# One transpose of K per step of an attention loop, moved from TensorE to VectorE and to transfers inside SBUF

## The chip, the cores and the metric

The kernel runs on one core of one Trainium2 chip. The metric is the device time of one execution in microseconds, the median of several runs: 2669.0 us before the change (three runs, 2667.27 to 2669.63 us).

## The reference, cut to what matters

The input is 2 x 1024 tokens of width 512, in float32. A block of linear attention with decay (32 heads of 128) and a gated feed-forward block follow one another, each between layer norms and with a residual. The attention part, as the reference has it:

```python
qkv = jax.nn.silu(hidden_states @ qkv_w.T)
...
def step(kv, blk):
    cq, ck, cv = blk
    scores = jnp.einsum('bhnd,bhmd->bhnm', cq, ck) * diag_decay
    intra = jnp.einsum('bhnm,bhmd->bhnd', scores, cv)
    inter = jnp.einsum('bhnd,bhde->bhne', cq * q_decay, kv)
    kv_next = kv * block_decay + jnp.einsum('bhnd,bhne->bhde', ck * k_decay, cv)
    return (kv_next, intra + inter)
...
normed = norm_w * xf.astype(attn.dtype)
gate = jax.nn.sigmoid(hidden_states @ gate_w.T)
return gate * normed @ out_w.T
```

K enters twice. The scores need it with the head's dimension on the partitions, as the projection leaves it. The state `kv_next` sums over the tokens of a block, so there K must have the tokens on the partitions: it has to be transposed, and scaled by `k_decay`.

## The kernel before, in words

**Tiling.** The heads go in 16 pairs, the 2048 tokens in four segments of 512 (`NSEG`, four chunks of 128 each). A pair with a segment is a step, `a`; there are 64. All engines are programmed by hand: each has its own list, with semaphores between them, and the order below is the order of each list. Loops over the pairs are hardware loops whose body holds four steps (`four_steps(i, ...)`, called i-th turn here, with `j` 0 to 3).

**TensorE** (`step`, L1260) interleaves step `a`'s attention with the projections of step `n = a + 1`. A projection is a `unit(n, seg, u)`, 12 matmuls of 512 columns or 24 of 256: units 0 and 1 make K of the two heads, 2 and 3 Q, 4 and 5 V, 6 and 7 the gate. The order in a step is: transposes and scores of head 0, unit 0, transposes and scores of head 1, unit 1, `contributions` (the new states, from `kd` and V), units 2 and 3, `attend` of both heads, units 4, 5 and 6, two `project_out`, unit 7, two more `project_out`. In `transposes_and_scores` (L1195) four 128x128 transposes of `k` go to the PSUM bank `kt_at[h]`, and then the four score matmuls follow. The same bank takes the attention output in `attend` (L1216) later in the step.

**ScalarE** (`step`, L548): `k_decay` (L532) copies `kt_at` with the decay as its scale into `kd`; then come the sigmoids of units 0 to 3 (`sigmoid`, L511), `square` (L538) of the two heads' attention outputs into `sq`, `gated_hi`, and the sigmoids of units 4 to 7. In each turn's step `j` = 3, `split_out_hi` stands between the squares and `gated_hi`.

**VectorE** (`step`, L860): `decay_scores` and `silu` of units 0 and 1 by turns, `update_state` of both heads, `silu` of 2 and 3, `gate` (L850, waits on the square), `silu` of 4 and 5, and `add_out` four times.

**GpSimd** (`attention`, L359): `query_decay`, `add_squares` (reads `sq`), `gated_lo` (the low half of the gated output, which `project_out` needs), in `j` = 3 also `split_out_lo` (L331), for which the first `project_out` of that step waits.

**SyncE** issues the transfers: four weight blocks, a table and the output weights for each pair (L259 to L290), each when its buffer has come free.

The last three steps (`late_step`, and the beginning of `last_step_and_ffn`) are written out apart and carry the middle layer norms besides; then the feed-forward part follows.

What a unit waits for is set here (L1174 to L1177): the V units wait for `silu` of the Q units, unit 6 for `silu` of unit 4, unit 7 for that of unit 5:

```python
                if u < 2:
                    wait(pe, sig_done, 8 * n - 1 + u)
                else:
                    pe.wait_ge(silu_done, 6 * n + u - 1)
```

Of the kernel before, what the change touches and what calls it, by code (L numbers as in the profile page):

```python
# [21 lines left out]
P = 128  # L22
# [23 lines left out]
CHECKS_PER_PAIR = 3  # L46
CHECK_PAIRS = WIDTH_CHECKS // CHECKS_PER_PAIR
F32R_EXACT = 2.0 ** 12

# [19 lines left out]
def sandwich_kernel(nc, x, w_attn, w_out, norm_w, tables, w_ints, ffn_scales, down_s, out):  # L69
    ctx = ExitStack()  # L70
    with ctx:
# [30 lines left out]
        nw = sb("nw", [P, 2])  # L102
        table = sb("table", [P, TAB])
# [8 lines left out]
        kt_at = [bank("kt_at0"), bank("kt_at1")]  # L112
        sc_st = [bank("sc_st0"), bank("sc_st1")]
        yp = [bank("yp0"), bank("yp1")]
        ln1_ring = kt_at + sc_st + yp
# [21 lines left out]
        kt_done = sem("kt_done")  # L137
# [68 lines left out]
        sumsq = sb("sumsq", [P, TOK], scope=two)  # L206
        two.close()
# [22 lines left out]
        ffn_ps = [proj_ps[0], proj_ps[1], kt_at[0], kt_at[1]]  # L230
# [11 lines left out]
        def chunk(c):  # L242
            return slice(c * P, (c + 1) * P)

# [13 lines left out]
        def _(sp):  # L258
# [25 lines left out]
            with sp.Fori(1, PAIRS) as p:  # L284
                attn_weights(p, KK)
                attn_weights(p, QQ)
                pair_tables(p)
                pair_out_weights(p)
                attn_weights(p, VV)
                attn_weights(p, GG)  # L290
# [12 lines left out]
            for s in range(NSEG):  # L303
                sp.wait_ge(proj_done, 8 * (STEPS - NSEG + s + 1))
                sp.dma_start(xres[s], x_tiles[s]).then_inc(xres_in[s], 16)
# [172 lines left out]
        def _(act):  # L478
# [53 lines left out]
            def k_decay(a, h):  # L532
                act.wait_ge(kt_done, 2 * a + h + 1)
                wait(act, contrib_done, 2 * a + h - 1)
                act.activation(kd[:, h].rearrange("p c d -> p (c d)"), kt_at[h][:, :], ACT.Copy,
                               scale=table[:, TAB_K + h:TAB_K + h + 1]).then_inc(kd_done, 1)

            def square(a, h):  # L538
                act.wait_ge(attn_done, 2 * a + h + 1)
                wait(act, ss_done, 2 * a + h - 1)  # L540
                act.activation(sq[:, h], kt_at[h][:, :], ACT.Square).then_inc(sq_done, 1)  # L541
# [218 lines left out]
        def _(dve):  # L760
# [89 lines left out]
            def gate(a, h):  # L850
                dve.wait_ge(sq_done, 2 * a + h + 1)
                dve.wait_ge(sig_done, 8 * a + 7 + h)
                dve.tensor_tensor(g[:, h], kt_at[h][:, :], g[:, h], ALU.mult).then_inc(gated_done, 1)
# [44 lines left out]
            for s in range(1, NSEG):  # L898
                silu(0, 2 * s - 2)
                silu(0, 2 * s - 1)  # L900
                if s == 1:
                    dve.wait_ge(x_in[3], 16)
                    norm_statistics(y_tile(3), 3)
# [61 lines left out]
            def late_step(a, seg, s):  # L965
# [7 lines left out]
                silu(n, 1)  # L973
                norm_scales(norm_a[s])
# [170 lines left out]
        def _(pe):  # L1145
# [70 lines left out]
            def attend(a, odd, h):  # L1216

                pe.wait_ge(qd_done, 2 * a + h + 1)
                pe.wait_ge(state_done, states_before(a, odd) + (h + 1) * (CH - odd))
                for c in range(CH):  # L1220
                    inter = c > 0 or odd
                    last = pe.matmul(kt_at[h][:, chunk(c)], v[:, c, h], pd[:, h, c],  # L1222
                                     start=True, stop=not inter)
                    if inter:
                        last = pe.matmul(kt_at[h][:, chunk(c)], state[:, h, (c - 1) % CH],  # L1225
                                         qd[:, h, chunk(c)], start=False, stop=True)
# [33 lines left out]
            def step(a, seg, n, pair_n=None, pair_a=None):  # L1260
                odd = seg % 2
                seg_n = (seg + 1) % NSEG
                transposes_and_scores(a, 0)
                unit(n, seg_n, 0, pair_n)
                transposes_and_scores(a, 1)
# [16 lines left out]
            def late_step(a, seg, s):  # L1282
# [3 lines left out]
                transposes_and_scores(a, 0)  # L1286
                unit(n, seg + 1, 0)
                sums_of_squares(s, yp[0])
                transposes_and_scores(a, 1)
# [74 lines left out]
            def last_step_and_ffn(narrow):  # L1364
# [11 lines left out]
                transposes_and_scores(last, 0)  # L1376
# [3 lines left out]
                transposes_and_scores(last, 1)  # L1380
# [109 lines left out]
```

## Time and profile before

| | before |
|---|---|
| median of three runs | 2669.0 us (2667.27 to 2669.63) |
| span of the profiled execution | 2665.3 us; its own time beside the span isn't listed, the median lies 3.7 us above the span |
| TensorE matmuls busy | 2616.9 us, 98% |
| TensorE weight loads busy | 2270.1 us, 85% |
| VectorE | 1095.1 us, 41% |
| ScalarE | 814.2 us, 31% |
| GpSimd | 849.6 us, 32% |
| granted TensorE clock | 0.995 of full speed on the mean |
| 16 DMA engines | 83.61 MB, 31 GB/s on the mean |

The span is the time from the first to the last instruction on the core. Busy time of matmuls is a sum in which neighbours overlap, so the share says that TensorE is hardly ever without work, not what one matmul costs: the cost of one is read from the distance of the starts, or from the chain of waits, in which each piece begins where the piece before it ends. All times of the trace count from the span's start.

### The profile page before, as it was taken

The page shows a single profiled execution, that of the slowest core. Times are in us where ns is not written, and L with a number is a line of the kernel's source. Part 1 is how long each engine was busy: PE and PEld are TensorE (multiplying, and loading weights), DVE is VectorE, ACT ScalarE, POOL GpSimd, SP SyncE. Part 2 cuts the span into 40 slices and gives each one's busy share as a digit, 9 for nine tenths or more (in the row PEclk, how much of TensorE's full clock was granted, in tenths as well). Part 3 has the DMA queues.
Part 4 walks back from the last instruction along what each step waited for, and adds up shares of the span by engine and source line. Part 5 has one row for each costly group of instructions (what it writes and reads, how often), then busy time and mean ns, then how long its engine had stood idle before and what let it go on. Part 6 is the DMA issues. An engine that isn't in the chain of part 4 may idle for free.

```text
span 2665.3 us, 40249 instructions
## 1 busy us (share of the span) xinstructions
PE 2616.9 (98%) x15072; PEld 2270.1 (85%) x15072; DVE 1095.1 (41%) x1945; ACT 814.2 (31%) x1251; POOL 849.6 (32%) x585
## 2 busy tenths in 40 slices
PE   7999999999999999999999999999999999999996
PEld 6888888888888888888888888888888888877774
DVE  6333333333333333333333333333333334655558
ACT  5232223222322222222223232222222224743333
POOL 3232333232323323232323332323223133434345
PEclk9999999999999999999999999999999999999998
DMA  3010101010100001010101010101000011101001
GB/s 127 17 40 17 36 17 40 17 40 17 40 17 29 24 11 39 17 40 17 40 13 40 17 40 17 40 17 37 20 20 25 9 48 32 53 24 40 32 24 63
DMA packets 31985, 83.61 MB, mean 31 GB/s; under 512 B 6096, under 2 KB 6096, under 8 KB 30928
## 3 DMA queue, kind: packets, MB, share of 16 engines
q1 hardware_dynamic: 25776, 70.07, 7.9%
q10 hardware_dynamic: 6048, 11.01, 1.4%
q8 instruction: 148, 2.42, 0.4%
q14 instruction: 13, 0.11, 0.0%
HBM read 76.87 MB, written 4.19 MB: 30 GB/s over the span
## 4 chain that ended last, share of the span: by engine, by line
PE 87%; issue 5%; POOL 3%; DVE 3%; ACT 2%; DMA 0%; POOLq 0%; SPq 0%; ACTq 0%; DVEq 0%
PE proj_ps L1157 54%; PE yp L1157 14%; PE sc_st L1202 4%; PE kt_at L1222 4%; PE kt_at L1225 4%; PE sc_st L1212 4%; PE kt_at L1199 2%; POOL h_lo L413 2%; PE kt_at L1157 1%; DVE stats L764 1%; POOL d_lo L408 0%; DVE y L1095 0%; ACT y L489 0%; POOL f_lo L403 0%; ACT L530 0%
## 5 line engine op out<-in xcount | busy, mean ns | idle before, releaser
L1157 PE MATMUL proj_ps<-x_hi,w_hi 128*128 128x512 f32 x1536 | 623.6, 406 | 1.7 <-DVE x_lo L799 1.4
L1157 PE MATMUL proj_ps<-x_hi,w_lo 128*128 128x512 f32 x1536 | 607.0, 395 | 0.0
L1157 PE MATMUL proj_ps<-x_lo,w_hi 128*128 128x512 f32 x1536 | 606.2, 395 | 0.0
L350 POOL TENSOR_TENSOR sumsq<-sumsq,sq 128x512 f32<-128x512 f32 x128 | 164.4, 1284 | 1234.0 <-ACT sq L541 1233.7
L858 DVE TENSOR_TENSOR y<-yp,y 128x512 f32<-128x512 f32 x256 | 176.9, 691 | 475.9 <-PE yp L1157 475.9
L1157 PEld LDWEIGHTS proj_ps<-x_hi,w_lo 128*128 128x128 f32 x1536 | 289.0, 188 | 68.9
L1157 PEld LDWEIGHTS proj_ps<-x_hi,w_hi 128*128 128x128 f32 x1536 | 290.1, 189 | 59.3 <-DVE x_lo L799 1.8
L1157 PEld LDWEIGHTS proj_ps<-x_lo,w_hi 128*128 128x128 f32 x1536 | 290.3, 189 | 57.7
L1157 PE MATMUL proj_ps<-w_hi,x_hi 128*128 128x256 f32 x1024 | 293.5, 287 | 2.0 <-DVE q L824 2.0
L1157 PE MATMUL proj_ps<-w_hi,x_lo 128*128 128x256 f32 x1024 | 288.3, 282 | 0.0
L1157 PE MATMUL proj_ps<-w_lo,x_hi 128*128 128x256 f32 x1024 | 287.7, 281 | 0.0
L341 POOL TENSOR_TENSOR qd<-q,table 128x512 f32<-128x512 f32 x128 | 162.7, 1293 | 226.2 <-DVE table L808 218.4
L824 DVE TENSOR_TENSOR k<-proj_ps,k 128x512 f32<-128x512 f32 x128 | 88.4, 691 | 312.0 <-ACT k L530 312.0
L1157 PE MATMUL yp<-ow_lo,g_hi 128*128 128x512 f32 x512 | 201.1, 393 | 0.0
L1157 PE MATMUL yp<-ow_hi,g_hi 128*128 128x512 f32 x512 | 200.7, 392 | 0.0
L1157 PE MATMUL yp<-ow_hi,g_lo 128*128 128x512 f32 x512 | 200.6, 392 | 0.0
L530 ACT ACTIVATE g<-proj_ps 128x512 f32<-128x512 f32 x128 | 76.6, 598 | 402.4 <-PE proj_ps L1157 402.4
L824 DVE TENSOR_TENSOR v<-proj_ps,v 128x512 f32<-128x512 f32 x128 | 88.5, 692 | 268.3 <-ACT v L530 268.2
L1157 PEld LDWEIGHTS proj_ps<-w_hi,x_hi 128*128 128x128 f32 x1024 | 192.9, 188 | 2.3 <-issue 2.3
L1157 PEld LDWEIGHTS proj_ps<-w_lo,x_hi 128*128 128x128 f32 x1024 | 193.0, 188 | 0.0
L1157 PEld LDWEIGHTS proj_ps<-w_hi,x_lo 128*128 128x128 f32 x1024 | 192.7, 188 | 0.0
L530 ACT ACTIVATE q<-proj_ps 128x512 f32<-128x512 f32 x128 | 76.3, 598 | 363.7 <-PE proj_ps L1157 363.6
(122 smaller groups left out, 4368.3 us busy)
## 6 DMA issues: line engine op xcount, KB each, us to landing
raw<-w_attn SPq DMA_DIRECT2D x64, 512.0 KB, 3.3
check<-w_ints ACTq DMA_DIRECT2D x42, 256.0 KB, 2.7
ow<-w_out SPq DMA_DIRECT2D x16, 512.0 KB, 3.3
fraw<-w_ints SPq DMA_DIRECT2D x7, 1024.0 KB, 4.8
table_stage<-tables SPq DMA_DIRECT2D x16, 258.0 KB, 2.7
x_again<-x SPq DMA_DIRECT2D x4, 1024.0 KB, 5.1
draw<-w_ints SPq DMA_DIRECT2D x7, 512.0 KB, 3.2
y<-x SPq DMA_DIRECT2D x3, 1024.0 KB, 11.2
```

What stands on the lines that cost most here:

```text
L341: pool.tensor_tensor(qd[:, h].rearrange("p (c n) -> p c n", c=CH), q[:, h].rearrange("p (c n) -> p c n", c=CH), decay.unsqueeze(1).to_broa ...
L350: pool.tensor_tensor(sumsq[:, tokens(seg)], sumsq[:, tokens(seg)], sq[:, h], ALU.add).then_inc(ss_done, 1)
L413: pool.tensor_tensor(h_lo[par][:, t], hid[:, t], h_hi[par][:, t].bitcast(F32), ALU.subtract).then_inc(hlo_done, 1)
L530: act.activation(dst, src, ACT.Sigmoid).then_inc(sig_done, 1)
L824: dve.tensor_tensor(dst, proj_ps[h][:, :], dst, ALU.mult).then_inc(silu_done, 1)
L858: dve.tensor_tensor(tile, yp[t % 2][:, :], tile, ALU.add).then_inc(yacc_done, 1)
L1157: last = pe.matmul(psum, s, m, start=n == 0, stop=n == len(terms) - 1)
L1199: last = pe.transpose(kt_at[h][:, chunk(c)], k[:, h, chunk(c)], ident[:, :])
L1202: last = pe.matmul(sc_st[h][:, chunk(c)], k[:, h, chunk(c)], q[:, h, chunk(c)], start=True, stop=True)
L1212: last = pe.matmul(sc_st[h][:, chunk(c)], kd[:, h, c], v[:, c, h], start=True, stop=True)
L1222: last = pe.matmul(kt_at[h][:, chunk(c)], v[:, c, h], pd[:, h, c], start=True, stop=not inter)
L1225: last = pe.matmul(kt_at[h][:, chunk(c)], state[:, h, (c - 1) % CH], qd[:, h, chunk(c)], start=False, stop=True)
```

## The change

K's four transposes a head leave TensorE, 512 instructions of 128x128 in the whole program. In their place:

- VectorE turns each head's `k` by 32x32 blocks (`turn_blocks`, two instructions of 128x512 a step), behind `silu` of unit 1 and ahead of `update_state`, one step earlier than `kd` is used. The result, `kt`, is a view of the buffer `sq`, which is free at that time.
- SyncE issues sixteen transfers a step (`swap_blocks`), each of 32 partitions x 1 KB from `kt` to a new tile `k_tok`, which put the turned blocks into their block row. Each block row of the destination has its semaphore, `kt_in[b]`.
- ScalarE's `k_decay` reads `k_tok` in SBUF in place of the PSUM bank, and waits for all sixteen transfers, once a step. `square` of head 0 also waits for them, since it overwrites `sq`, out of which they read: for those of step `a + 1`, which were issued in the same step.
- On TensorE the wait for `gated_done` moves from the scores to `attend`. The bank `kt_at` is now `at_ps`, and holds the attention output alone.
- The order of SyncE's weight transfers is written anew around the swaps. SBUF's scratch area for DMA descriptors is halved.

```diff
+        k_tok = sb("k_tok", [P, QUADS, 2, CH, QUAD])
...
+        kt = sq[:, :, :].rearrange("p h n -> p (h n)").rearrange("p (b h c d) -> p b h c d",
+                                                                   b=QUADS, h=2, c=CH)
...
+            def swap_blocks(n):
+                sp.wait_ge(blocks_done, 2 * n + 2)
+                wait(sp, kd_done, 2 * n)
+                for b in range(QUADS):
+                    for i in range(QUADS):
+                        sp.dma_start(k_tok[quad(b), i], kt[quad(i), b]).then_inc(kt_in[b], 16)
+
+            def four_steps(i, more):
+                for j in range(NSEG):
+                    swap_blocks(4 * i + 2 + j)
+                    if j == 1:
+                        attn_weights(i + 1, VV)
+                        attn_weights(i + 1, GG)
+                        if more:
+                            attn_weights(i + 2, KK)
+                            attn_weights(i + 2, QQ)
+                    if j == 3 and more:
+                        pair_tables(i + 2)
+                        pair_out_weights(i + 2)
...
             def k_decay(a, h):
-                act.wait_ge(kt_done, 2 * a + h + 1)
+                if h == 0:
+                    for b in range(QUADS):
+                        act.wait_ge(kt_in[b], 16 * QUADS * (a + 1))
                 wait(act, contrib_done, 2 * a + h - 1)
-                act.activation(kd[:, h].rearrange("p c d -> p (c d)"), kt_at[h][:, :], ACT.Copy,
+                act.activation(kd[:, h].rearrange("p c (i d) -> p i c d", i=QUADS), k_tok[:, :, h],
+                               ACT.Copy,
                                scale=table[:, TAB_K + h:TAB_K + h + 1]).then_inc(kd_done, 1)
 
             def square(a, h):
                 act.wait_ge(attn_done, 2 * a + h + 1)
                 wait(act, ss_done, 2 * a + h - 1)
+                if h == 0 and not (isinstance(a, int) and a == STEPS - 1):
+                    for b in range(QUADS):
+                        act.wait_ge(kt_in[b], 16 * QUADS * (a + 2))
...
+            def turn_blocks(n, h):
+                dve.wait_ge(silu_done, 6 * n + h + 1)
+                if h == 0:
+                    wait(dve, ss_done, 2 * (n - 1))
+                    if isinstance(n, int) and n == 1:
+                        for b in range(QUADS):
+                            dve.wait_ge(kt_in[b], 16 * QUADS)
+                dve.transpose(kt[:, :, h],
+                              k[:, h].rearrange("p (c b t) -> p b c t", c=CH, b=QUADS))\
+                    .then_inc(blocks_done, 1)
...
                 for h in range(2):
                     decay_scores(a, h)
                     silu(n, h)
+                turn_blocks(n, 0)
+                turn_blocks(n, 1)
                 update_state(a, odd, 0)
                 update_state(a, odd, 1)
...
-            def transposes_and_scores(a, h):
+            def scores(a, h):
                 pe.wait_ge(silu_done, 6 * a + 3 + h)
-                wait(pe, gated_done, 2 * a + h - 1)
-                for c in range(CH):
-                    last = pe.transpose(kt_at[h][:, chunk(c)], k[:, h, chunk(c)], ident[:, :])
-                last.then_inc(kt_done, 1)
                 for c in range(CH):
                     last = pe.matmul(sc_st[h][:, chunk(c)], k[:, h, chunk(c)], q[:, h, chunk(c)],
                                      start=True, stop=True)
...
             def attend(a, odd, h):
 
                 pe.wait_ge(qd_done, 2 * a + h + 1)
+                wait(pe, gated_done, 2 * a + h - 1)
...
     nc = bacc.Bacc("TRN2", target_bir_lowering=False, num_devices=1,
+                   dynamic_dma_scratch_size=DMA_SCRATCH)
```

The same turn and swap are also written for the first steps (`swap_blocks(0)`, `swap_blocks(1)`) and the late ones.

**Order on TensorE**, in the loop over the pairs, at the scores of head 1 of a step. Before:

```order
L1157 MATMUL proj_ps0<-x_lo,w_hi 128x512
L1157 MATMUL proj_ps0<-x_hi,w_lo 128x512
L1196 REGISTER_ALU
L1199 MATMUL kt_at1<-ident,k 128x128 x4
L1202 MATMUL sc_st1<-q,k 128x128 x4
L1157 MATMUL proj_ps1<-x_hi,w_hi 128x512
```

and with the change:

```order
L1217 MATMUL proj_ps0<-x_lo,w_hi 128x512
L1217 MATMUL proj_ps0<-x_hi,w_lo 128x512
L1256 REGISTER_ALU
L1258 MATMUL sc_st1<-q,k 128x128 x4
L1217 MATMUL proj_ps1<-x_hi,w_hi 128x512
L1217 MATMUL proj_ps1<-x_lo,w_hi 128x512
```

The four transposes between unit 0 and the scores are gone, and nothing has come in their place. (`x4` counts matmuls of the program; the chip runs each float32 score matmul as two, so the trace has eight.)

**Order on VectorE**, in the same loop, from `silu` of unit 1 on, with the change:

```order
L862 REGISTER_ALU
L865 TENSOR_TENSOR k<-proj_ps,k 128x512
L869 ISA
L875 STREAM_TRANSPOSE sq<-k 128x4x128
L869 REGISTER_ALU
L875 STREAM_TRANSPOSE sq<-k 128x4x128
L64 ISA
L899 SCALAR_TENSOR_TENSOR state<-state,table,sc_st 128x128
```

Before, the row of the state followed that of `k` directly. The two turns are put ahead of six (in steps of the other parity eight) small instructions of `update_state`.

**Order on SyncE**, the beginning of its loop over the pairs with the change (here `sq` is the buffer under the view `kt`):

```order
L321 UNCONDITIONAL_BRANCH
L321 ISA
L300 DMA k_tok<-sq 32x256 x16
L296 ISA
L300 DMA k_tok<-sq 32x256 x16
L64 ISA
L272 ISA
L272 DMA raw<-w_attn 128x1024
```

Seven transfers a pair have become seventy-one, and the sixteen of one step stand without another instruction between them.

## Rows read from the trace of the kernel before

**Rows 1.** The page's busy time; busy time by windows, of the steady steps (PE, PEld, DVE, ACT, POOL).

```profile
PE 2616.9 (98%) x15072; PEld 2270.1 (85%) x15072; DVE 1095.1 (41%) x1945; ACT 814.2 (31%) x1251; POOL 849.6 (32%) x585
...
66.60:2146.00 2079.40, 2079.40 (x12402) 1825.72 (x12400) 758.15 (x1352) 562.58 (x895) 622.45 (x427) 1.00 0.09 27
```

**Rows 2.** The groups of instructions by line: K's transposes (count, busy, mean ns, idle).

```profile
L1199 PE MATMUL kt_at<-ident,k 128*128 128x128 f32 x512 | 76.9, 272 | 0.2 <-issue 0.2
```

**Rows 3.** The chain of waits through one steady step (start us, us, what).

```profile
1012.01 0.44 PE kt_at L1199 x4
1012.44 0.89 PE sc_st L1202 x8
...
1016.13 1.34 PE sc_st L1212 x12
1017.47 5.60 PE proj_ps L1157 x24
...
1026.65 8.47 PE proj_ps L1157 x60
1035.12 2.76 PE yp L1157 x12
```

**Rows 4.** VectorE's copies of the table (ns min/median/max, first and last start us).

```profile
L808 DVE COPY table<-table_stage x16: 421/429/5437, 43.9 to 2181.5; 128x516 f32<-128x516 f32 x16
```

**Rows 5.** VectorE in order of time, around silu of unit 1 of that step.

```profile
1016.80 0.69 DVE L824 TENSOR_TENSOR k<-proj_ps,k 128x512 f32<-128x512 f32 x1 [2.73 <-ACT k L530]
1017.41 2.25 DVE L846 SCALAR_TENSOR_TENSOR state<-state,table,sc_st 128x128 f32<-128x128 f32 x6
```

**Rows 6.** SyncE's issues in order of time; two groups of transfers (KB, us to landing).

```profile
0.75 1.81 SPq L274 DMA_DIRECT2D y<-x  x4
...
2146.58 0.34 SPq L301 DMA_DIRECT2D fraw<-w_ints  x1
2146.97 0.43 SPq L302 DMA_DIRECT2D fs_stage<-ffn_scales  x1
...
raw<-w_attn SPq DMA_DIRECT2D x64, 512.0 KB, 3.3
out<-y SPq DMA_DIRECT2D x8, 256.0 KB, 2.0
y<-x SPq DMA_DIRECT2D x4, 256.0 KB, 3.3
```

**Rows 7.** ScalarE and GpSimd in the same step, from the squares to the low half.

```profile
1024.90 0.60 ACT L541 ACTIVATE sq<-kt_at 128x512 f32<-128x512 f32 x1 [1.19 <-PE kt_at L1225]
1026.68 0.60 ACT L541 ACTIVATE sq<-kt_at 128x512 f32<-128x512 f32 x1 [1.19 <-PE kt_at L1225]
1029.53 0.60 ACT L530 ACTIVATE v<-proj_ps 128x512 f32<-128x512 f32 x1 [0.77 <-PE proj_ps L1157]
...
1025.57 1.27 POOL L350 TENSOR_TENSOR sumsq<-sumsq,sq 128x512 f32<-128x512 f32 x1 [13.91 <-ACT sq L541]
1028.60 2.53 POOL L356 TENSOR_TENSOR g_lo<-g,g_hi 128x512 fp32r<-128x512 f32 x2
```

**Rows 8.** The next step (`j` = 3): ScalarE's squares, GpSimd's low half of the output weights.

```profile
1060.65 0.60 ACT L541 ACTIVATE sq<-kt_at 128x512 f32<-128x512 f32 x1 [0.96 <-PE kt_at L1225]
1062.22 0.60 ACT L541 ACTIVATE sq<-kt_at 128x512 f32<-128x512 f32 x1 [0.97 <-PE kt_at L1225]
...
1066.86 2.39 POOL L333 TENSOR_TENSOR ow_lo<-ow,ow_hi 128x1024 fp32r<-128x1024 f32 x1
```

**Rows 9.** The two late steps: silu of unit 1, and what follows it.

```profile
2226.09 0.69 DVE L824 TENSOR_TENSOR k<-proj_ps,k 128x512 f32<-128x512 f32 x1 [2.72 <-ACT k L530]
...
2235.96 0.60 ACT L541 ACTIVATE sq<-kt_at 128x512 f32<-128x512 f32 x1 [1.19 <-PE kt_at L1225]
...
2264.97 0.69 DVE L824 TENSOR_TENSOR k<-proj_ps,k 128x512 f32<-128x512 f32 x1 [2.73 <-ACT k L530]
2266.49 0.18 DVE L791 RECIPROCAL rstd<-stdev 128x4 f32<-128x4 f32 x1 [0.83 <-ACT stdev L482]
```

More of the change, by code:

```diff
@@ L46 @@
 CHECKS_PER_PAIR = 3
+QUAD = 32
+QUADS = P // QUAD
 CHECK_PAIRS = WIDTH_CHECKS // CHECKS_PER_PAIR
 F32R_EXACT = 2.0 ** 12
+DMA_SCRATCH = 8192
 ACT = mybir.ActivationFunctionType
@@ L111, in sandwich_kernel @@
         proj_ps = [bank("proj_ps0"), bank("proj_ps1")]
-        kt_at = [bank("kt_at0"), bank("kt_at1")]
+        at_ps = [bank("at_ps0"), bank("at_ps1")]
         sc_st = [bank("sc_st0"), bank("sc_st1")]
         yp = [bank("yp0"), bank("yp1")]
-        ln1_ring = kt_at + sc_st + yp
+        ln1_ring = at_ps + sc_st + yp
         x_in = [sem(f"x_in{s}") for s in range(NSEG)]
@@ L136, in sandwich_kernel @@
         proj_done = sem("proj_done")
-        kt_done = sem("kt_done")
+        blocks_done = sem("blocks_done")
+        kt_in = [sem(f"kt_in{b}") for b in range(QUADS)]
         score_done = sem("score_done")
@@ L229, in sandwich_kernel @@
         xres = [x_again[:, :, s * SEG:(s + 1) * SEG] for s in range(NSEG)]
-        ffn_ps = [proj_ps[0], proj_ps[1], kt_at[0], kt_at[1]]
+        ffn_ps = [proj_ps[0], proj_ps[1], at_ps[0], at_ps[1]]
         ffn_ps_first = [proj_ps[0], proj_ps[1], yp[0], yp[1]]
@@ L243, in chunk, with quad @@
             return slice(c * P, (c + 1) * P)
+        def quad(b):
+            return slice(b * QUAD, (b + 1) * QUAD)
         norm_a = [NSEG + 2 * s for s in range(NSEG)]
@@ L283, in _ @@
             pair_out_weights(0)
[L284 to L290, printed above, removed]
+            def swap_blocks(n):
[16 more added lines that the diff above has]
+                        pair_out_weights(i + 2)
+            swap_blocks(0)
+            attn_weights(1, KK)
+            attn_weights(1, QQ)
+            pair_tables(1)
+            swap_blocks(1)
+            pair_out_weights(1)
+            with sp.Fori(0, PAIRS - 2) as i:
+                four_steps(i, True)
+            four_steps(PAIRS - 2, False)
             def ffn_weights(n):
@@ L303, in _ @@
             for s in range(NSEG):
+                if s >= 2:
+                    swap_blocks(STEPS - 4 + s)
                 sp.wait_ge(proj_done, 8 * (STEPS - NSEG + s + 1))
@@ L900, in _ @@
                 silu(0, 2 * s - 1)
+                if s == 1:
+                    turn_blocks(0, 0)
+                    turn_blocks(0, 1)
                 if s == 1:
@@ L973, in late_step @@
                 silu(n, 1)
+                turn_blocks(n, 0)
+                turn_blocks(n, 1)
                 norm_scales(norm_a[s])
@@ L1221, in attend @@
                     inter = c > 0 or odd
-                    last = pe.matmul(kt_at[h][:, chunk(c)], v[:, c, h], pd[:, h, c],
+                    last = pe.matmul(at_ps[h][:, chunk(c)], v[:, c, h], pd[:, h, c],
                                      start=True, stop=not inter)
                     if inter:
-                        last = pe.matmul(kt_at[h][:, chunk(c)], state[:, h, (c - 1) % CH],
+                        last = pe.matmul(at_ps[h][:, chunk(c)], state[:, h, (c - 1) % CH],
                                          qd[:, h, chunk(c)], start=False, stop=True)
@@ L1262, in step @@
                 seg_n = (seg + 1) % NSEG
-                transposes_and_scores(a, 0)
+                scores(a, 0)
                 unit(n, seg_n, 0, pair_n)
-                transposes_and_scores(a, 1)
+                scores(a, 1)
                 unit(n, seg_n, 1, pair_n)
@@ L1285, in late_step @@
                 wait(pe, xlo_done, TILES + CH * s)
-                transposes_and_scores(a, 0)
+                scores(a, 0)
                 unit(n, seg + 1, 0)
                 sums_of_squares(s, yp[0])
-                transposes_and_scores(a, 1)
+                scores(a, 1)
                 unit(n, seg + 1, 1)
@@ L1375, in last_step_and_ffn @@
                 pe.wait_ge(xlo_done, TILES + 2 * CH)
-                transposes_and_scores(last, 0)
+                scores(last, 0)
                 sums_of_squares(2, yp[0])
@@ L1379, in last_step_and_ffn @@
                 project(0, 0, ffn_ps_first)
-                transposes_and_scores(last, 1)
+                scores(last, 1)
                 contributions(last, 1, 0)
```

6 lines of the change are left out of this document (3 added, 3 removed).

## Prediction

> **What bounds the kernel now.** First the busy times. TensorE is busy 98% of the span, and in the window of the steady steps all 2079.4 of 2079.4 us; no other engine passes 41% [rows 1]. So what TensorE does not have to do shortens the program, as long as nothing it waits for comes late. Second the cost of the thing removed. The group of K's transposes gives 272 ns for one, 512 of them [rows 2]. That is a duration with overlap in it. The chain of waits, whose pieces don't overlap, gives 0.44 us for the four of one head, ahead of 0.89 us for eight score matmuls [rows 3]. Third, the idle time ahead of that group is 0.2 us in all [rows 2]: no wait hides in it. Fourth, since the new path runs over four engines, the time at which each wants its input, from the timelines of one steady step.
>
> **What is taken from TensorE.** 64 steps x 2 heads x 0.44 us = 56.3 us. It would be less if the scores, now straight behind a unit, began later than the transposes do. The contributions stand behind a unit already: twelve matmuls in 1.34 us, 0.112 each, and the scores behind the transposes take 0.111 each [rows 3]. So the change of neighbour costs nothing that shows; I allow 54 to 59 us. The wait for the gated output that moves to attend costs nothing: that output belongs to the step before, whose projections out of it are done by then.
>
> [...]
>
> **What VectorE gets.** Two turns of 128x512 a step, which this trace doesn't have. The nearest rows are a copy of 516 elements (0.43 us at the median) and a product of 512 (0.69 us) [rows 4, 5]. A turn of 32x32 blocks reads with a stride and can't be taken to run as fast as the plain copy, so I take 0.69, 1.4 us for both; ends 0.86 and, if it took twice a product, 2.8. They stand behind silu of unit 1, which ends at 1017.49, and ahead of the state's six updates of 2.25 us [rows 5]. The states would be ready at 1018.9 + 2.3 = 1021.2; attend wants them at 1017.47 + 5.60 = 1023.07 [rows 3]. That cover lasts even for 2.8 us (1022.5). The longest of those copies took 5437 ns where 429 is the median [rows 4]; it is the first, beside GpSimd's clearing of `y`. In the steady step GpSimd has been idle for 13.91 us at 1025.57 [rows 7], so around 1017.5 there is nothing to collide with, and I charge nothing.
>
> **The sixteen transfers and who waits.** k_decay of the next step wants them a whole half step later, over 20 us: nothing there. The wait that matters is `square` of head 0, in the same step, since it overwrites their source. Blocks ready: 1018.9. Pace of issue: two transfers outside a loop start 0.39 us apart (2146.58 and 2146.97), four at the start of the program take 1.81, 0.45 each; one issue itself is 0.33 to 0.34 [rows 6]. Landing after issue: 2.0 us for the smallest and quickest, 256 KB, 3.3 for 512 KB [rows 6]; ours are 32 KB each, so 2.0. The last lands at 1018.9 + 15 x 0.39 + 2.0 = 1026.8. The square of head 0 starts at 1024.90 today [rows 7]. It will be **late by 1.9 us**. Ends: 0.33 apart and turns of 0.43 give 1025.3, late by 0.4; 0.45 apart and 3.3 to landing give 1028.95, late by 4.0; with turns of 2.8 us as well, 5.4.
>
> Is that covered? I follow what stands behind the square on ScalarE, x being its lateness. The second square starts 0.5 us behind it instead of at 1026.68, so most of x is taken up by time in which ScalarE waits today. The gates on VectorE follow each by 0.7 and 0.6, the high halves end at 3.3, and the V sigmoid can start about 2.7 behind the first square: 1027.6 + x, today 1029.53 [rows 7]. Sigmoid and silu take 0.6 and 0.7, so silu of unit 4 ends at 1028.9 + x. Unit 6 waits for it. It starts one unit (24 matmuls in 5.60, so 2.80) ahead of the projections out, 1035.12 - 2.80 = 1032.3 [rows 3]. **Cover: x up to 3.4.** The other branch: GpSimd's two sums and two low halves (2.53 the last pair) end 5.7 behind the square, 1030.6 + x, against 1035.12 [rows 3, 7]: x up to 4.5. In the turn's step `j` = 3 the output weights' low half is in that branch. It ends at 1066.86 + 2.39 = 1069.25 with the second square at 1062.22; with the squares back to back that would be 1060.65 + 0.5 + x, so it ends at 1068.2 + x; the projections out come some 10 us behind the first square, as in the step before (1024.90, 1035.12), so at about 1070.7 [rows 3, 7, 8]. Cover in these 15 steps: x up to 2.5. My 1.9 is inside all three.
>
> SyncE is free for each swap: the weight transfers of `j` = 1 wait for GpSimd's low halves, but GpSimd is idle from 1025.57 - 13.91 = 1011.7 on [rows 7], so the last of these is over 7 us ahead of the next swap. The prologue takes one pair of turns on VectorE behind ScalarE's table loads: nothing.
>
> **Late steps.** Here ScalarE is in the chain already. In the first, silu of unit 1 ends at 2226.78, blocks are ready 1.4 later, the last lands 7.9 after that, 2236.0; the second square, in the chain, moves from 2235.96 to about 2236.6: +0.6. In the second, the reciprocal of the layer norm has to stand behind the turns: 2265.66 + 1.4 against 2266.49, +0.5 [rows 9]. Sum +1.1, ends 0 and 8.
>
> **Sum.** 2665.3 - 56.3 + 1.1 = 2610.1 us of span. The median lies 3.7 above the span of the profiled execution and I keep that: **2614 us**, -2.1%. Range of this case alone: 2610 to 2623.
>
> **The rivals.**
>
> - Partly uncovered. x lies between 2.5 and 4.1. At 3.3 only the fifteen steps with `j` = 3 stall, by 0.8: +12, 2626 us. At 4.0 they stall by 1.5 and the other 48 by 0.6: +51, 2665. For it: the two pace rows of the prologue. Against: these transfers are an eighth of the size there.
> - **Slower.** One mechanism: the last of the sixteen lands so late that the square's lateness goes through silu of unit 4 to unit 6. It decides from 48 (x - 3.4) + 15 (x - 2.5) = 55, so x = 4.1: a last landing 10 us after the blocks are ready. With all upper ends (turns 1.4 each, 0.45 apart, 3.3 to landing) x = 5.4, and TensorE stalls 48 x 2.0 + 15 x 2.9 = 140 us: 2614 + 140 = 2754. For it: no row shows a transfer within SBUF, nor sixteen issues on end. Against: it needs every end at once.
> - Transfers that don't overlap. If each took its 2.0 us before the next began, the last would land 32 us after the blocks, x = 26, and 63 steps would stall by about 23: some 4060 us. Against: four of 256 KB are issued within 1.81 us and land a median 3.3 us after issue [rows 6], which four in turn could not. [...]
> - The whole length of a transpose comes free: 512 x 0.272 = 139 us, 2531 us. The chain's 0.44 for four speaks against it.
>
> That the change doesn't do what it says can be left out: the order on TensorE has the scores straight behind the unit, and nothing in the transposes' place.
>
> **Chances.** Forecast 0.68; partly uncovered 0.16 (0.04 of it within 0.2% of before); slower 0.12; no overlap 0.03; whole length 0.01. Faster by over 0.2% (5.3 us, about what a measurement of this kernel can tell from no change): 0.68 + 0.12 + 0.01 = 0.81; the same 0.04; slower 0.15. The range takes the first case and the better half of the second, with a little room below: 2608 to 2645.
>
> **What would show it.** Right: no transposes in the chain, 0.44 us less between the unit and the end of the scores; turns near 0.69 us; first square about 2 us later against unit 2, second right behind it; the last transfer at 8 us from the blocks; unit 6 without a wait. Wrong: TensorE idle before a unit of proj_ps, released by silu, or before the projections out, released by a low half; ScalarE's square released by a DMA more than 3.4 us late; turns over 1.4 us.

## The result, and the profile after

| | before | changed |
|---|---|---|
| median of 4 runs | 2668.14 us (2666.80 to 2669.63) | 2807.66 us (2802.31 to 2814.48) |
| profiled execution: span | 2665.3 us | 2800.5 us |
| TensorE busy | 2616.9 us (98%) | 2614.1 us (93%) |
| profiled execution: mean granted TensorE clock | 0.995 | 0.981 (the four runs: 0.978 to 0.983) |

The changed kernel takes 1.0525 times as long, 95% interval 1.0512 to 1.0538: 139.5 us slower where 54 us less was forecast. The first view to read is again the page's busy time, then the chain of waits by engine and by line, and the groups.

```profile
PE 2614.1 (93%) x14560; PEld 2249.3 (80%) x14560; DVE 1151.2 (41%) x2073; ACT 797.3 (28%) x1251; POOL 845.6 (30%) x585
...
PE 44%; SPq 17%; issue 17%; DVE 7%; ACT 5%; POOL 5%; DMA 4%; ACTq 0%; DVEq 0%; POOLq 0%
PE proj_ps L1217 25%; SPq L300 17%; PE yp L1217 14%; DMA k_tok<-sq 4%; PE sc_st L1258 4%; DVE sq L875 2%; POOL h_lo L448 2%; DVE v L865 1%; ACT k L565 1%; ACT sq L582 1%; DVE g L906 1%; ACT v L565 1%; PE at_ps L1217 1%; POOL ow_lo L368 1%; POOL sumsq L385 1%
...
L1217 PE MATMUL proj_ps<-x_hi,w_hi 128*128 128x512 f32 x1536 | 644.9, 420 | 121.2 <-DVE v L865 119.5
...
L1217 PE MATMUL yp<-ow_hi,g_hi 128*128 128x512 f32 x512 | 201.7, 394 | 8.5 <-POOL ow_lo L368 8.5
```

512 transposes have gone (15072 matmuls in [rows 1], 14560 here), yet TensorE's busy time is almost what it was, and it is no longer busy throughout. 17% of the chain is now the issuing of transfers by SyncE (`SPq L300` is the swap). Two groups of matmuls have an idle time, 119.5 us behind V's silu and 8.5 us behind the low half of the output weights: the two places that the prediction named as signs of being wrong. The table of waits says who waits for the transfers themselves:

```profile
ACT sq L582 <- DMA k_tok<-sq: 395.0, 63, 7.3
PE proj_ps L1217 <- DVE v L865: 119.5, 61, 2.8
PE yp L1217 <- POOL ow_lo L368: 8.5, 9, 1.0
PE sc_st L1225 <- ACT xn L524: 10.1, 3, 4.8
```

(Total us, times, longest.) ScalarE's square waits 63 times, 6.3 us on average. The last line is a third place where TensorE stands still, ahead of the layer norm's transposes in the late steps; it is taken up where the prediction is judged. Then the swap's and the turn's own rows: ns at least, at the median, at most, first and last start; and from issue to landing.

```profile
L300 SPq DMA_DIRECT2D k_tok<-sq x1024: 507/591/1645, 26.9 to 2405.8; - x171
...
DMA to landing us min/median/max: 1.7/1.8/3.1
...
L875 DVE STREAM_TRANSPOSE sq<-k x128: 667/686/704, 25.5 to 2395.2; 128x512 f32<-128x512 f32 x128
```

One issue keeps SyncE for 0.59 us. The chain through one steady step (start us, us, what) shows what sixteen of them make:

```profile
1072.69 0.68 DVE sq L875
1073.39 0.52 SPq L300
1073.95 0.59 SPq L300
...
1082.19 0.59 SPq L300
1082.82 1.84 DMA k_tok<-sq
...
1084.76 0.61 ACT sq L582
...
1085.48 0.70 DVE g L906
...
1087.35 0.59 ACT v L565
1087.96 0.70 DVE v L865
...
1088.70 3.06 PE proj_ps L1217 x12
```

The blocks are ready at 1073.37. The first issue starts at 1073.39 and the sixteenth at 1082.82, 0.63 us apart from start to start, and this last transfer lands at 1084.66, **11.3 us after the blocks**. From there the chain runs square, gate, high half, V's sigmoid and silu, and only then unit 6. The timelines of the same step put numbers on the lateness (in brackets the idle time before):

```profile
1084.76 1.09 ACT L582 ACTIVATE sq<-at_ps 128x512 f32<-128x512 f32 x2 [6.48 <-DMA k_tok<-sq]
...
1088.70 0.50 PE L1217 MATMUL proj_ps<-x_hi,w_hi 128*128 128x512 f32 x1 [1.79 <-DVE v L865]
```

ScalarE waits 6.48 us where it waited 1.19 [rows 7], so the square is late by x = 5.3; both squares now stand back to back, as foretold. TensorE stands still for 1.79 us.

A second loss shows one step earlier, where the same unit took longer. TensorE's timeline, then busy time and granted clock by windows (the clock is the third number from the end):

```profile
1050.42 0.78 PE L1217 MATMUL proj_ps<-x_hi,w_hi 128*128 128x512 f32 x1 [1.85 <-DVE v L865]
1051.00 0.63 PE L1217 MATMUL proj_ps<-x_lo,w_hi 128*128 128x512 f32 x1
```

```profile
1051.40:1052.40 1.00, 1.00 (x4) 0.78 (x3) 0.40 (x1) 0.62 (x1) 1.00 (x2) 0.50 0.00 0
1053.40:1054.40 1.00, 1.00 (x4) 0.77 (x4) 0.00 (x0) 0.00 (x0) 1.00 (x1) 0.76 0.00 0
```

Behind the idle time TensorE's granted clock is 0.50, called the lower level from here on; up to 1050.4 it was 1.00. Matmuls follow each other at 0.43 us instead of 0.23, and the clock is back at 1.00 near 1053.9 (about half of the second window, 0.76 on the mean, is at the lower level). In the chain this piece of twelve matmuls is 4.62 us long:

```profile
1050.42 4.62 PE proj_ps L1217 x12
```

against 3.06 at 1088.70, where the clock stayed up, and 2.80 where nothing waited. In the 61 steps that stall so, the trace has 20 such falls, each at the end of a stall or within 1 us of it, and each 3.4 us long.

### The profile page after: what moved, and what is told of

It reads as the page before. It is cut to its first block, busy times and chain, and to the rows that moved or that the text cites. A ratio compares the mean times of both kernels' runs of the same rounds, so it can differ in the third digit from the quotient of the medians.

```text
span 2800.5 us, 40792 instructions
## 1 busy us (share of the span) xinstructions
PE 2614.1 (93%) x14560; PEld 2249.3 (80%) x14560; DVE 1151.2 (41%) x2073; ACT 797.3 (28%) x1251; POOL 845.6 (30%) x585
## 4 chain that ended last, share of the span: by engine, by line
PE 44%; SPq 17%; issue 17%; DVE 7%; ACT 5%; POOL 5%; DMA 4%; ACTq 0%; DVEq 0%; POOLq 0%
PE proj_ps L1217 25%; SPq L300 17%; PE yp L1217 14%; DMA k_tok<-sq 4%; PE sc_st L1258 4%; DVE sq L875 2%; POOL h_lo L448 2%; DVE v L865 1%; ACT k L565 1%; ACT sq L582 1%; DVE g L906 1%; ACT v L565 1%; PE at_ps L1217 1%; POOL ow_lo L368 1%; POOL sumsq L385 1%
## 5 line engine op out<-in xcount | busy, mean ns | idle before, releaser
L1217 PE MATMUL proj_ps<-x_hi,w_hi 128*128 128x512 f32 x1536 | 644.9, 420 | 121.2 <-DVE v L865 119.5
L1217 PE MATMUL proj_ps<-x_lo,w_hi 128*128 128x512 f32 x1536 | 619.8, 404 | 0.0
L1217 PE MATMUL proj_ps<-x_hi,w_lo 128*128 128x512 f32 x1536 | 618.3, 403 | 0.0
L1217 PEld LDWEIGHTS proj_ps<-x_hi,w_hi 128*128 128x128 f32 x1536 | 297.5, 194 | 193.9 <-DVE v L865 131.7
L1217 PEld LDWEIGHTS proj_ps<-x_hi,w_lo 128*128 128x128 f32 x1536 | 297.6, 194 | 71.9
L1217 PEld LDWEIGHTS proj_ps<-x_lo,w_hi 128*128 128x128 f32 x1536 | 299.2, 195 | 60.8
L906 DVE TENSOR_TENSOR g<-at_ps,g 128x512 f32<-128x512 f32 x128 | 82.4, 686 | 379.7 <-ACT sq L582 379.7
L1279 PE MATMUL at_ps<-pd,v 128*128 128x128 f32 x1024 | 187.2, 275 | 0.0
```

The costliest lines, as they stand in the source:

```text
L906: dve.tensor_tensor(g[:, h], at_ps[h][:, :], g[:, h], ALU.mult).then_inc(gated_done, 1)
L1217: last = pe.matmul(psum, s, m, start=n == 0, stop=n == len(terms) - 1)
L1279: last = pe.matmul(at_ps[h][:, chunk(c)], v[:, c, h], pd[:, h, c], start=True, stop=not inter)
```

## The experiments

Theory after the result: SyncE's pace of issue makes the square late, and its lateness passes through V's silu to unit 6. Rivals: the turns on VectorE or the traffic itself cost the time; the form of the transfers (32 partitions each) makes them slow; the two issuing queues share something, so that the pace can't be improved; the clock makes a good part of the loss. Diffs are against the changed kernel.

### What the removed transposes are worth, and whether the wait is the loss

Kernel e2_gain: no turns, no swaps, no waits for them. It leaves out K's part of the state: `k_decay` reads a cleared buffer.

```diff
             def swap_blocks(n):
-                sp.wait_ge(blocks_done, 2 * n + 2)
-                wait(sp, kd_done, 2 * n)
-                for b in range(QUADS):
-                    for i in range(QUADS):
-                        sp.dma_start(k_tok[quad(b), i], kt[quad(i), b]).then_inc(kt_in[b], 16)
+                return
...
             def turn_blocks(n, h):
...
+                return
```

> No turns, no transfers and no waits for them; k_decay reads a buffer that is cleared once, so K's part of the state is left out. It prices what leaves TensorE by itself. Theory A: before minus 56 us, 2612 +- 3. If the scores behind a unit cost more than the transposes did, above 2620; if a whole transpose of 272 ns comes free, 2530.

Measured 2611.80 us (2611.11 to 2611.93), ratio to before 0.9789 (0.9772 to 0.9805). 2668.13 - 2611.80 = 56.3 us: the sum's 64 x 2 x 0.44. The new order of the weight transfers, the halved scratch area and the moved wait for `gated_done` are all in this kernel, so they cost nothing that shows.

Kernel e1_own: everything of the change, but the turned blocks get a buffer of their own, and the square's wait is gone with its reason.

```diff
-DMA_SCRATCH = 8192
+DMA_SCRATCH = 4096
...
+        kt = sb("kt", [P, QUADS, 2, CH, QUAD])
...
             def square(a, h):
-                if h == 0 and not (isinstance(a, int) and a == STEPS - 1):
-                    for b in range(QUADS):
-                        act.wait_ge(kt_in[b], 16 * QUADS * (a + 2))
...
             def turn_blocks(n, h):
-                    wait(dve, ss_done, 2 * (n - 1))
-                    if isinstance(n, int) and n == 1:
-                        for b in range(QUADS):
-                            dve.wait_ge(kt_in[b], 16 * QUADS)
+                    for b in range(QUADS):
+                        wait(dve, kt_in[b], 16 * QUADS * n)
```

> The turned blocks get a buffer of their own, and the square waits for no transfer; turns, sixteen transfers and their issues stay. Theory A (the loss is the square's wait for the last of sixteen transfers issued 0.63 us apart, and what TensorE loses behind it, idle and at the lower clock): 2612 to 2622 us, no idle time of TensorE ahead of unit 6. Rival B (the turns on VectorE or the traffic in SBUF slow the other engines by themselves): stays above 2700, the stalls of TensorE stay. Rival C (half of it is issue time on SyncE that delays the weight transfers): 2640 to 2700, with waits on w_lo or ow_lo.

Measured 2614.49 us (2610.93 to 2616.49), ratio 0.9795 (0.9779 to 0.9812), clock 0.995. Its issues, and a square of a steady step:

```profile
L299 SPq DMA_DIRECT2D k_tok<-kt x1024: 507/591/1816, 26.6 to 2224.6; - x171
```

```profile
1002.50 0.60 ACT L578 ACTIVATE sq<-at_ps 128x512 f32<-128x512 f32 x1 [1.19 <-PE at_ps L1276]
```

The issues are as slow as before, and the square waits 1.19 us for TensorE again, as in [rows 7]. With all turns and all 1024 transfers in place the kernel is within 3 us of the one without any. So neither the turns nor the traffic cost anything that shows beyond these 3 us: the whole loss, 193 us against this kernel, hangs on one wait for a shared buffer.

### The pace, in doses

Kernel e3_twelve leaves away four of the sixteen transfers, the blocks on the diagonal, which are then missing in the result. The counts in the waits are adapted.

```diff
                 for b in range(QUADS):
                     for i in range(QUADS):
+                        if i == b:
+                            continue
                         sp.dma_start(k_tok[quad(b), i], kt[quad(i), b]).then_inc(kt_in[b], 16)
```

> Twelve transfers a step in place of sixteen: the four diagonal blocks aren't moved (left out of the result). Theory A: the last lands 4 x 0.63 = 2.5 us earlier, the idle time of some 2 us ahead of unit 6 goes in most steps and the low clock with it: 2615 to 2645. Rival B: the loss goes with the number of transfers and of bytes, a quarter of it: about 2760.

Measured 2639.05 us (2638.06 to 2643.13), ratio 0.9891 (0.9874 to 0.9907), clock 0.993. Its waits and one piece of its chain:

```profile
ACT sq L584 <- DMA k_tok<-sq: 238.7, 63, 5.1
PE yp L1222 <- POOL ow_lo L370: 14.3, 16, 0.9
```

```profile
1054.54 2.35 POOL ow_lo L370
...
1057.01 3.02 PE yp L1222 x12
```

A quarter less takes 169 us of the 196 away. The square now waits 3.8 us on average, x is about 2.7, and unit 6 waits for 1.3 us in the whole program (cover 3.4). What is left over is found by comparing the starts of each step's scores with those of e2_gain, in the two profiled executions, 31 us apart: 19 us in the sixteen steps with `j` = 3 (1.1 to 1.3 each, through the low half of the output weights), 9 us in the two late steps, 4 us elsewhere.

Kernel e5_hbm keeps sixteen transfers of the same size and target, but reads them from HBM, out of a weight tensor, so K's part of the state is wrong in it.

```diff
-                        sp.dma_start(k_tok[quad(b), i], kt[quad(i), b]).then_inc(kt_in[b], 16)
+                        sp.dma_start(k_tok[quad(b), i].rearrange("p h c d -> p (h c d)"),
+                                     w_out[0, quad(i), 0, 0:256]).then_inc(kt_in[b], 16)
```

> The sixteen transfers read 32 rows x 1 KB of a weight tensor in HBM in place of the turned blocks in SBUF; number, size, destination, order and every wait are kept (K's part of the state is then not K's). What makes an issue 0.59 us? If SBUF as the source: issues return to 0.33 to 0.45 us, the last lands some 2 to 3 us earlier although HBM answers later, and the time falls to 2615 to 2700. If sixteen issues back to back cost that whatever they move: 0.59 us again and 2800 to 2850.

```profile
L300 SPq DMA_DIRECT2D k_tok<-w_out x1024: 310/421/1680, 26.2 to 2242.3; - x171
...
DMA to landing us min/median/max: 1.6/1.7/3.3
```

```profile
ACT sq L583 <- DMA k_tok<-w_out: 234.9, 63, 5.0
PE yp L1218 <- POOL ow_lo L369: 12.4, 16, 1.0
```

Measured 2638.80 us (2635.87 to 2642.26), ratio 0.9897 (0.9880 to 0.9913). From HBM an issue takes 0.42 us, and issues start 0.46 us apart. The landing is about the same, 1.7 us against 1.8; that HBM answers later, as the expectation says, didn't show at 32 KB. The square's wait (3.7 us) is that of e3_twelve, and so is the time, with sixteen transfers instead of twelve. Lateness decides, however it comes about. Here, too, lies the error of the forecast: its rows were transfers from HBM or to it. For those its upper end (0.45 us apart) nearly holds; its middle value (0.39) was too low even for them.

### Is it the form?

Kernel e4_four_wide: four transfers over all 128 partitions, 128 KB each. The blocks end in the wrong partitions, so it prices the form and isn't a version to use. The counts in the waits are adapted.

```diff
-                    for i in range(QUADS):
-                        sp.dma_start(k_tok[quad(b), i], kt[quad(i), b]).then_inc(kt_in[b], 16)
+                    sp.dma_start(k_tok[:, b], kt[:, b]).then_inc(kt_in[b], 16)
```

> Four transfers a step of 128 partitions x 1 KB in place of sixteen of 32 partitions: the same bytes, straight down instead of across block rows (the blocks end in the wrong partitions). Theory A: last landing some 8 us earlier, the square not held up, 2610 to 2620. Rival B (traffic): as slow as the change, about 2800. It also tells what the 0.59 us of an issue hang on: 0.33 to 0.43 us if on the form of 32 partitions, 0.59 or more if on SBUF as the source.

```profile
L299 SPq DMA_DIRECT2D k_tok<-sq x256: 464/601/2186, 26.2 to 2213.1; - x128
...
DMA to landing us min/median/max: 1.9/2.1/4.2
```

Measured 2613.60 us (2611.29 to 2618.82), ratio 0.9803 (0.9787 to 0.9819). The same bytes in a quarter of the issues: nothing is late. One issue costs 0.60 us here as well, so the price doesn't hang on 32 partitions or on 32 KB. What the slow issues have in common is that both ends lie in SBUF; with one end in HBM they took 0.42 us (the source, e5_hbm) and 0.33 us (the target, the write of e8_dram below).

### Two queues

Kernel e6_two_queues gives eight of the sixteen to ScalarE, between its sigmoids of units 1 and 2.

```diff
             def swap_blocks(n):
...
-                for b in range(QUADS):
+                for b in range(QUADS if isinstance(n, int) and n >= STEPS - 2 else 2):
...
+            def swap_half(n):
+                act.wait_ge(blocks_done, 2 * n + 2)
+                wait(act, kd_done, 2 * n)
+                for b in (2, 3):
+                    for i in range(QUADS):
+                        act.dma_start(k_tok[quad(b), i], kt[quad(i), b]).then_inc(kt_in[b], 16)
```

> Half of the sixteen transfers are issued by ScalarE, between its sigmoids of units 1 and 2, the other half by SyncE at the same time; the same buffer, the same waits, all work kept. Theory A (the issues of one engine in a row are the delay): last landing 8 x 0.63 + 1.8 = 6.8 us behind the blocks, square late by 1, no stall: 2612 to 2625. Rival D (the DMA engines or a unit shared by both queues takes 0.6 us for each transfer): no gain, 2790 to 2830, and issues on both engines of over 1 us.

Measured 2646.69 us (2644.96 to 2649.08), ratio 0.9923 (0.9906 to 0.9939). SyncE, then ScalarE, in the same step:

```profile
1008.10 4.99 SPq L300 DMA_DIRECT2D k_tok<-sq  x8
```

```profile
1008.11 5.33 ACTq L594 DMA_DIRECT2D k_tok<-sq  x8
1013.62 1.09 ACT L565 ACTIVATE q<-proj_ps 128x512 f32<-128x512 f32 x2 [7.48 <-issue]
```

Both queues issue side by side, 0.62 and 0.67 us each. SyncE alone started its issues 0.63 us apart, so the second queue costs the first nothing that shows, and no unit shared by both took 0.6 us for each transfer. The last transfer lands 6.6 us behind the blocks, as expected (6.8), but the time is 2647 us and not 2612 to 2625. Against e2_gain the profiled execution is 35 us longer. 15 us are in the steps with `j` = 3, 1.0 each: the 5.3 us come out of ScalarE's own time, Q's sigmoids are late and stand back to back, and in those steps that reaches the low half of the output weights, and through it TensorE. 12 us are in the two late steps, where SyncE still issues all sixteen (the last lands 12.2 us behind the blocks). 8 us come before the first step, whose scores start at 55.7 us against 47.4; the first eight issues on ScalarE stand in the prologue, but that they are the cause isn't shown.

Here the issuing engine paid for its transfers: 5.0 us on SyncE, which has nothing else to do, and 5.3 us on ScalarE, which has.

### How much of it is the clock

Kernel e7_fill puts eight matmuls that compute nothing ahead of unit 6, e9_fill_four puts four, and e10_change_again is the changed kernel beside the latter.

```diff
                 unit(n, seg_n, 5, pair_n)
+                for _ in range(8):
+                    pe.matmul(sc_st[0][:, :], x_hi[:, 0, chunk(CH * seg_n)], x_hi[:, 0, tokens(seg_n)],
+                              start=True, stop=True)
                 unit(n, seg_n, 6, pair_n)
```

> The change, with eight matmuls of 512 columns whose result nobody reads ahead of unit 6 in each step, 8 x 0.23 = 1.9 us: they fill idle time. If the idle time alone is the loss: 2808 +- 10. If TensorE's fall to the lower clock after the idle time is a part of it (mean granted clock 0.981 against 0.995): that part comes back, clock 0.99 or more, 2765 to 2785.

> Four idle matmuls of 512 columns instead of eight stand ahead of unit 6, in 61 steps: 61 x 4 x 0.234 = 57 us of work that computes nothing, all of it inside the 2.8 us that TensorE waits there on average, so the fill itself lengthens nothing. Theory (part of the loss is TensorE's clock, which falls after the idle time): the wait that is left is near 121 - 57 = 64 us, the mean granted clock rises from 0.981 to 0.99 or more, and the program gets SHORTER although it does more: 2807.7 less 15 to 35 us, 2773 to 2793. Rival (the long matmuls behind a stall are nothing but their late start, and the mean clock is only a figure): within 5 us of the changed kernel. A second rival (the wait is set by silu, and the fill delays it through TensorE's queue): longer than the changed kernel.

> The changed kernel itself, beside the one with four idle matmuls on the same chip, so that the two can be compared directly: 2802 to 2815 us, clock near 0.98.

| kernel | us | ratio to before | clock | falls in the 61 steps |
|---|---|---|---|---|
| e7_fill | 2798.82 (2797.63 to 2802.25) | 1.0494 (1.0477 to 1.0512) | 0.992 | 0 |
| e9_fill_four | 2804.27 (2802.16 to 2815.61) | 1.0512 (1.0498 to 1.0527) | 0.988 | 8 |
| e10_change_again | 2810.23 (2801.57 to 2811.72) | 1.0522 (1.0507 to 1.0538) | 0.979 | 23 |

The clock came back as the theory said, the time hardly did: e9_fill_four is within its uncertainty of the changed kernel, not 15 to 35 us below, and e7_fill lies 9 us below the changed kernel's first measurement, where 23 to 43 were expected. (The expectation for e9_fill_four also calls 2.8 us the average wait; that is the longest, the average is 1.96.) Three things explain it.

First, in a stall the filling only takes the stall's place. In e7_fill, the step behind a `j` = 3 step has no stall left, and the filling itself is in the chain, 1.83 us where 1.79 stood:

```profile
1156.25 5.69 PE proj_ps L1217 x48
1161.94 1.83 PE sc_st L1333 x8
1163.77 3.02 PE proj_ps L1217 x12
```

Second, with the filling the square itself comes later. In one step of its chain one of the sixteen issues takes 1.29 us in place of 0.59, and the waits for the transfers grow from 395.0 us in all (e7_fill, then e9_fill_four):

```profile
1190.13 1.29 SPq L300
```

```profile
ACT sq L582 <- DMA k_tok<-sq: 415.8, 63, 7.7
ACT sq L582 <- DMA k_tok<-sq: 412.6, 63, 8.1
```

In two of four steps of e7_fill the last transfer lands 12.0 and 12.3 us behind the blocks (medians) instead of 11.3. Waits for silu and filling together are 29.5 + 61 x 1.83 = 141.1 us in e7_fill and 80.6 + 61 x 0.92 = 136.7 in e9_fill_four, against 119.5 without filling: 21.6 and 17.2 us more, about the 20.8 and 17.6 us that the square waits longer. Why single issues stretch isn't known; e1_own, which has no filling, has sixteen of over 0.9 us, the changed kernel seven, e7_fill 26.

Third, a fall doesn't always cost its length. Of the 20 falls, seven are in steps with `j` = 3. There the projections out would have waited 0.95 us for the low half anyway, and without falls they do: the waits for the low half rise from 8.5 us (9 times) to 15.6 and 15.4 (16 times).

Against these 21.6 + 7.1 and 17.2 + 6.9 us stands what the clock gave back. Twelve matmuls behind a stall take 4.62 us with a fall and 3.06 without (both in the changed kernel's chain), so a fall costs 1.56 us, and 20 falls fewer are 31 us, 12 fewer 19. The two nearly cancel, which is the result measured. What the lower level took from TensorE in the changed kernel, its late part included, is (0.995 - 0.981) x 2800 = **39 us**, 31 of it in the steps; what it adds to the time is some 7 us less, by the waits that it hides. Both figures are read from the traces; no run isolates them.

### A version that beats both

Kernel e8_dram replaces the sixteen transfers by one that writes the turned blocks to HBM, and four that read them back as block rows. The square waits for the one write only.

```diff
+        kt_out = sem("kt_out")
...
+        kt_dram = nc.dram_tensor("kt_dram", (P, 2 * SEG), F32, kind="Internal").ap()
+        kt_blocks = kt_dram.rearrange("(i p) (b f) -> b p i f", i=QUADS, b=QUADS)
...
+                sp.dma_start(kt_dram[:, :], sq[:, :, :].rearrange("p h n -> p (h n)")).then_inc(kt_out, 16)
+                sp.wait_ge(kt_out, 16 * (n + 1))
                 for b in range(QUADS):
-                    for i in range(QUADS):
-                        sp.dma_start(k_tok[quad(b), i], kt[quad(i), b]).then_inc(kt_in[b], 16)
+                    sp.dma_start(k_tok[quad(b)].rearrange("p i h c d -> p i (h c d)"),
+                                 kt_blocks[b]).then_inc(kt_in[b], 16)
...
             def square(a, h):
...
-                    for b in range(QUADS):
-                        act.wait_ge(kt_in[b], 16 * QUADS * (a + 2))
+                    act.wait_ge(kt_out, 16 * (a + 2))
```

> The swap goes through HBM: one transfer of 128 partitions x 4 KB writes the turned blocks out, and when it has landed four transfers of 32 partitions x 4 KB read them back in block order; the square waits for the first alone. Five issues in place of sixteen, no buffer more in SBUF. Theory A: the source is free 0.6 + 2.5 us after the turns, ahead of the square: 2611 to 2618, faster than both kernels. If traffic to HBM or the order of SyncE's queue matters: above 2625.

Measured 2611.57 us (2610.78 to 2613.04), ratio 0.9792 (0.9775 to 0.9808), which is the time of e2_gain. SyncE in one step, then the write's and the reads' rows, each with its time to landing:

```profile
1028.21 0.34 SPq L301 DMA_DIRECT2D kt_dram<-sq  x1
1030.84 1.73 SPq L304 DMA_DIRECT2D k_tok<-kt_dram  x4
```

```profile
L301 SPq DMA_DIRECT2D kt_dram<-sq x64: 326/334/343, 26.0 to 2211.2; - x64
...
DMA to landing us min/median/max: 2.6/2.6/4.9
...
L304 SPq DMA_DIRECT2D k_tok<-kt_dram x256: 302/432/1667, 28.7 to 2215.2; - x128
...
DMA to landing us min/median/max: 2.5/2.9/3.9
```

The source is free 2.6 us after the issue instead of 11.3 us after the blocks. The reads take their time where K has a whole half step. Like e1_own it computes all that the reference does; unlike it, it needs no further buffer in SBUF.

## Why the prediction was wrong

- **The gain**, 56.3 us: right to the tenth (e2_gain). The last rival, a gain of the full length of a transpose (139 us), is ruled out by it.
- **The turns**, 0.69 us: 0.686 at the median. They delay nothing (e1_own).
- **The pace of issue was the step that failed**: "the last lands at 1018.9 + 15 x 0.39 + 2.0". The starts are 0.63 us apart, above even the upper end of 0.45. 15 x 0.24 = 3.6 us is the whole of the error in the landing. The range's upper end was the highest row of transfers with one end in HBM, though the text itself said that no row showed one within SBUF. A bound has to be looser where the kind of thing differs, and this term is multiplied by fifteen.
- **The landing**, 2.0 us: 1.8 at the median. That the transfers overlap was right too: sixteen in turn, at 1.8 us each, would have landed 29 us behind the blocks, and the last landed at 11.3. With the same bytes in four issues instead of sixteen nothing is late (e4_four_wide, 2613.6 us). What joining saves in this kernel is issue time (0.59 us each), not landing time (2.1 us there, 1.8 here).
- **x**: 5.3 us measured, 1.9 forecast. It is near the slower rival's "all upper ends" of 5.4, reached by one term alone, while the turns and the landing stayed near their middle values.
- **The cover**: x up to 3.4 for unit 6 held. The stall at x = 5.3 should be 1.9 us, and TensorE waits 119.5 / 61 = 1.96 us on average; at x = 2.7 (e3_twelve, e5_hbm) it waits for little more than 1 us in the whole program. The 2.5 us for the `j` = 3 steps were less good: at x = 2.7 the waits for the low half should be 0.2 us each and are 0.8 to 0.9, so that cover is nearer 1.8.
- **The slower rival's price** was 2754 us at x = 5.4, and 2807.7 was measured: a second term was missing, what a stall costs beyond its length. Against e2_gain, whose span is 2610.1 with TensorE busy for 2558.4, the changed kernel's 190.4 us more divide into 134.7 us of idle time (119.5 ahead of unit 6, 8.5 ahead of the projections out, and some 8 more in the late steps), near the 140 of that rival, and 55.7 us in which matmuls take longer. Of the latter, 39 us are the clock's, and some 15 us are the first matmuls behind each stall (3.06 instead of 2.80 us for twelve, 61 times). In this kernel a stall cost more than its length.
- **The late steps** were a second error, +1.1 us in the sum with 8 as the upper end: in the changed kernel the two take 12.3 us more than in e2_gain. There the square stands ahead of the middle layer norm in ScalarE's list, and TensorE waits for it where it hardly waited before. The changed kernel, twice, then e2_gain:

```profile
2369.50 1.94 PE L1225 MATMUL sc_st<-ident,xn 128*128 128x128 f32 x8 [4.81 <-ACT xn L524]
2414.16 1.94 PE L1225 MATMUL sc_st<-ident,xn 128*128 128x128 f32 x8 [4.71 <-ACT xn L524]
```

```profile
2186.62 1.33 PE L1209 MATMUL sc_st<-ident,xn 128*128 128x128 f32 x8 [0.27 <-ACT xn L520]
```

The granted clock is at its lower level around the end of both waits (0.51 in 2368 to 2375 us and in 2412.4 to 2419.3 us). The kernels without a late square (e1_own, e8_dram) lose less than 1 us there, e3_twelve at half the lateness still 9.

- **The chances**: the mechanism that came true, its place and its threshold (a last landing over 10 us after the blocks) stood among the rivals with 0.12, "needs every end at once". It needed one.

Open: why an issue with both ends in SBUF takes 0.59 us (the runs show that it does so for 32 and for 128 partitions and on two queues, not what the queue does meanwhile), why single issues stretch to 1.0 to 1.8 us, and why the clock falls behind some stalls of 1.8 us and not behind others.

## What to carry to other kernels

Count the issues that stand between a buffer's filling and its reuse, multiply them by the measured duration of one issue of the same kind of source and target, and only then add one landing; if no row has that kind, let the upper bound be loose and give the rival the weight. When many small moves hold a buffer that others wait for, free the buffer with one large transfer (here to HBM, free after 2.6 us instead of 11.3), or give the moves a buffer of their own (e1_own). Where a bound engine stalls each step, price the first work behind the stall as well (here twelve matmuls in 3.06 us instead of 2.80, and in 4.62 where the clock fell).

## What the runs showed of the hardware

- An issue on SyncE took 0.59 us from SBUF to SBUF (0.60 with 128 partitions and 128 KB, e4_four_wide), 0.42 to 0.43 from HBM to SBUF when they followed each other (e5_hbm, e8_dram), 0.33 from SBUF to HBM (e8_dram). ScalarE issued at about the same pace as SyncE (0.617 us against 0.592, medians), at the same time (e6_two_queues).
- The sixteen transfers landed 1.8 us after their issue at the median, and from HBM (e5_hbm) 1.7 us.
- A turn of 32x32 blocks on VectorE over 128x512 float32 took 0.686 us, as long as a product of two such tiles (0.69) [rows 5] and longer than a copy of 128x516 (0.429) [rows 4].
- Behind idle times of 1.6 to 2.9 us a step TensorE's granted clock fell from 1.00 to 0.50, for 3.4 us, in 20 of 61 steps in one execution and 23 in another (the changed kernel, e10_change_again); with eight matmuls in that idle time (e7_fill), in none.
- A way through HBM and back (e8_dram: 2.6 us out, 2.9 us in at the median) was hidden as a whole, and was faster for the waiting engine than sixteen moves within SBUF: the source was free 2.6 us after the issue instead of 11.3 us after the blocks.
